# The grouped convolution of a mixer as two plain float32 products side by side, on one Trainium2 core

## What is computed

```python
p = hidden_states @ in_proj_w.T                 # 256 -> 2 x 512
h, gate = (p[..., :I], p[..., I:])
gate = jax.nn.silu(gate)
hc = jnp.transpose(h, (0, 2, 1))
conv = jax.lax.conv_general_dilated(hc, conv_w, window_strides=(1,), padding=[(K - 1, 0)], feature_group_count=G, ...)
h = jnp.transpose(conv + conv_b[None, :, None], (0, 2, 1)) * gate
residual = h
hn = _layernorm(h, ln_g, ln_b)
m = jax.nn.silu(hn @ fc_w.T + fc_b) @ cproj_w.T + cproj_b
return (m + residual) @ out_w.T
```

## Time and profile before

| | |
|---|---|
| runs | 2779.84 us median (2778.41 to 2786.03) |
| the profiled execution's own time | 2780.32 us |
| its span | 2778.2 us |
| mean granted TensorE clock | 0.929 of full speed |
| TensorE busy (matmul) | 2366.8 us, 85% |
| VectorE / ScalarE / GpSimd busy | 1525.3 us (55%) / 1282.9 us (46%) / 518.5 us (19%) |
| mixer stage | from the start to about 764 us |

### The profile page before, as it was taken

The page is one execution under the profiler, slowest core; times in us unless marked ns, Lnnn a source line. Parts: engine busy times, 40 slices in busy tenths (PEclk is TensorE's granted clock), DMA queues, the critical chain, the costliest instruction groups (busy, mean ns, idle before and its releaser), DMA issues. The chain is left out here.

```text
span 2778.2 us, 45597 instructions
## 1 busy us (share of the span) xinstructions
PE 2366.8 (85%) x15266; PEld 1791.3 (64%) x15266; DVE 1525.3 (55%) x3440; ACT 1282.9 (46%) x2197; POOL 518.5 (19%) x429
## 2 busy tenths in 40 slices
PE   7999999999869999647888888888888877159997
PEld 6777777777658888525555555555555557149996
DVE  4544444444345454355666666666666646766664
ACT  2444444444445554624555555555555545024442
POOL 0111111111111111510110000100011013026663
PEclk8999999999989999768999999999999988569998
DMA  3200000000010000122333223223232207435542
GB/s 112 88 0 0 0 0 0 0 0 0 0 31 0 0 0 0 38 69 68 73 75 80 73 74 79 74 70 80 69 77 71 70 24 263 118 111 127 126 89 34
DMA packets 121392, 157.18 MB, mean 57 GB/s; under 512 B 24800, under 2 KB 102000, under 8 KB 121200
## 3 DMA queue, kind: packets, MB, share of 16 engines
q1 hardware_dynamic: 106992, 130.90, 17.2%
q0 software_dynamic: 14336, 25.44, 4.7%
HBM read 96.78 MB, written 58.98 MB: 56 GB/s over the span
## 5 line engine op out<-in xcount | busy, mean ns | idle before, releaser
L1461 DVE TENSOR_REDUCE at_top<-psum 128x1 f32<-128x512 f32 (+3 forms) x1024 | 447.2, 485 | 300.3 <-PE psum L1237 299.7
L1588 ACT ACTIVATE at_probs<-psum 128x512 f32<-128x512 f32 (+1 forms) x768 | 365.8, 530 | 346.5 <-PE psum L1255 344.5
L1235 PE MATMUL psum<-at_k_stack,at_q_stack 96*128 96x512 bf16 (+3 forms) x1024 | 295.4, 315 | 128.0 <-DMA at_k_stack<-qk_parts 72.5
L1253 PE MATMUL psum<-at_q_stack,at_k_stack 98*128 98x512 bf16 (+3 forms) x1024 | 288.9, 309 | 23.1 <-ACT at_probs L1588 16.8
L1235 PEld LDWEIGHTS psum<-at_k_stack,at_q_stack 96*128 96x128 bf16 x1024 | 103.1, 101 | 229.2 <-DVE at_top L1461 102.3
L1237 PE MATMUL psum<-at_mask_q,at_ident_b 128*128 128x128 bf16 x1024 | 206.3, 227 | 0.0
L1255 PE MATMUL psum<-at_mask_k,at_ident_b 128*128 128x128 bf16 x1024 | 202.4, 224 | 0.0
L1253 PEld LDWEIGHTS psum<-at_q_stack,at_k_stack 98*128 98x128 bf16 x1024 | 102.5, 100 | 115.1 <-issue 44.2
L1271 PE MATMUL psum<-at_probs,at_values 128*32 128x512 f32 (+3 forms) x2048 | 151.1, 436 | 0.9 <-ACT at_probs L1588 0.9
L570 POOL TENSOR_TENSOR y<-y,mean 128x512 f32<-128x512 f32 x64 | 83.2, 1333 | 364.8 <-ACT mean L623 364.8
L2312 POOL DMA_INDIRECT out<-ex_result,slot_tokens x64 | 119.6, 1869 | 102.8 <-DVE ex_result L2444 88.2
(11 more groups left out here) (404 smaller groups left out, 6142.1 us busy)
## 6 DMA issues: line engine op xcount, KB each, us to landing
qk_parts<-at_q_parts SPq DMA_DIRECT2D x96, 128.0 KB
qk_parts<-at_k_parts SPq DMA_DIRECT2D x96, 128.0 KB
at_q_stack<-qk_parts SPq DMA_DIRECT2D x64, 192.0 KB
at_k_stack<-qk_parts SPq DMA_DIRECT2D x64, 192.0 KB
x_residual<-in_x SPq DMA_DIRECT2D x16, 512.0 KB, 8.4
at_q_stack<-qk_parts SPq DMA_DIRECT2D x64, 128.0 KB
at_k_stack<-qk_parts SPq DMA_DIRECT2D x64, 128.0 KB
token_rows<-ro_h_tok SPq DMA_DIRECT2D x16, 512.0 KB, 3.0
```

The source lines that it names most:

```text
L1235: pe.matmul(out, q_stack[0:STACK, h, qt * P:(qt + 1) * P], k_stack[0:STACK, h, 0:w], start=True, stop=True)
L1253: pe.matmul(bank(bk)[:, col:col + w], k_stack[0:STACK + N_SHIFT, h, kt * P:(kt + 1) * P], q_stack[0:STACK + N_SHIFT, h, kt * P:T], start=T ...
L1461: dve.tensor_reduce(top[:, h, qt:qt + 1], bank(MAX0 + n % 2)[:, col:col + w], AX.X, ALU.max).then_inc(mxr.sem, 1)
L1588: act.activation(probs[:, slot(h), 512 * f:512 * f + w], bank(f)[:, 0:w], ACT.Exp).then_inc(ex.sem, 1)
```

## The change

The convolution is laid out anew. A new tile `h_taps` holds h in plain float32 twice per block: in copy g the 64 partitions of group g hold h itself, and the other 64 partitions hold the same group's h shifted by one token. One contraction over 128 partitions then covers two taps of one group of 64 channels, and the four taps take two such products per group. The two groups of a block write the two halves of a PSUM bank through two column tiles of TensorE (`tile_position=(0, 64 g)`). ScalarE copies the lower 64 partitions of the product h, once in place and once across to the upper partitions; VectorE does the mirror image. No high and low parts are made for the convolution. Beside this:

- the convolution's weights go by four DMAs straight to their place; their staging area, the two splits and the semaphores of these are gone;
- VectorE computes two of the four pieces of `dev`, GpSimd the other two;
- the narrow matmuls for the squares stand ahead of the first `out` matmul (before: after six), and the `quads` matmul after nine `out` matmuls (before: after twelve);
- VectorE splits `fc` before it copies h, not after;
- batches 4 to 15 of x are loaded one after the other, each when the one before has arrived.

```diff
-        w_conv = pair("w_conv", [P, IK * TAPS, P])
+        w_conv = sb("w_conv", [P, 2 * IK * 2, HALF])
-        h_s = pair("h", [P, IK, TAPS - 1 + T])
+        h_st = sb("h_taps", [P, IK, 2, TAPS - 1 + T])
...
-            sp.dma_start(f_conv, t["conv_blocks"].rearrange("n p m -> p n m")).then_inc(conv_in, 16)
+            for g, side in enumerate(SIDES):
+                for rows, tap in ((SIDES[g], 1), (SIDES[1 - g], 0)):
+                    sp.dma_start(w_conv[rows, 2 * IK * g:2 * IK * (g + 1), :],
+                                 t["conv_blocks"][tap::2, side, side].rearrange("n p m -> p n m")).then_inc(small, 16)
...
-            for b in range(EARLY, NB):
-                load_x(b, x_rest.sem)
+            for i in range(NB):
+                b = i - 1 + EARLY
+                if EARLY <= b < NB:
+                    if b == EARLY:
+                        sp.wait_ge(folded, 1)
+                        sp.wait_ge(mod_done, 2)
+                        sp.wait_ge(lo, len(PIECES))
+                    else:
+                        sp.wait_ge(*x_rest(b - 1 - EARLY, 16))
+                    load_x(b, x_rest.sem)
...
                 if m == 3:
-                    pe.wait_ge(*hl(i, 1))
+                    pe.wait_ge(*ha(i, 2))
+                    pe.wait_ge(*hd(i, 2))
...
             if not first:
-                pe.wait_ge(*hl(i, 3))
+                pe.wait_ge(*ha(i, 6))
+                pe.wait_ge(*hd(i, 6))
                 pe_turn_out(pe, i - 1)
-            pe.wait_ge(*hl(i, 4))
+            pe.wait_ge(*ha(i, 8))
+            pe.wait_ge(*hd(i, 8))
             if first:
-                pe.wait_ge(lo, CONV_W + 1)
+                pe.wait_ge(small, 13 * 16)
...
-                for k in range(TAPS):
-                    last = product3(pe, bank(CONV + m), [w[:, m * TAPS + k, :] for w in w_conv],
-                                    [h[:, m, k:k + T] for h in h_s], k == 0, k == TAPS - 1)
+                for k in range(2):
+                    for g, side in enumerate(SIDES):
+                        last = pe.matmul(bank(CONV + m)[side, :], w_conv[:, 2 * IK * g + 2 * m + k, :],
+                                         h_st[:, m, g, 1 + 2 * k:1 + 2 * k + T], start=(k == 0), stop=(k == 1),
+                                         tile_position=(0, HALF * g), skip_group_check=True)
...
-                    if m == 0 and k == 2:
+                    if m == 0 and k == 0:
                         pe.wait_ge(*sq(i, 4))
...
-                    if m == 1 and k == 0:
+                    if m == 0 and k == 3:
                         pe.wait_ge(*vqs(i, 1))
...
-        def dve_h_lo(dve, i, first):
+        def dve_keep_h(dve, i, first):
             for m in range(IK):
-                dve.wait_ge(*hh(i, m + 1))
-                dve.tensor_tensor(h_s[1][:, m, TAPS - 1:], bank(H0 + m), h_s[0][:, m, TAPS - 1:].bitcast(F32),
-                                  ALU.subtract).then_inc(hl.sem, 1)
+                dve.wait_ge(*hp(i, m + 1))
+                dve.tensor_copy(h_st[SIDES[1], m, 1, TAPS - 1:], bank(H0 + m)[SIDES[1], :]).then_inc(hd.sem, 1)
+                dve.tensor_copy(h_st[SIDES[0], m, 1, TAPS:], bank(H0 + m)[SIDES[1], 0:T - 1]).then_inc(hd.sem, 1)
...
             if not last_batch:
                 dve_hT_lo(dve, i + 1, False)
+            dve.wait_ge(*ms(i, 1))
+            for m in range(2, IK):
+                dve.tensor_tensor(dev[:, m, :], y[:, m, :], mean[:, :], ALU.subtract).then_inc(fc0.sem, 1)
...
-            if not last_batch:
-                dve_h_lo(dve, i + 1, False)
             for m in range(DK):
                 dve.wait_ge(*fh(i, m + 1))
                 dve.tensor_tensor(fc_s[1][:, m, :], fc[:, m, :], fc_s[0][:, m, :].bitcast(F32),
                                   ALU.subtract).then_inc(fl.sem, 1)
+            if not last_batch:
+                dve_keep_h(dve, i + 1, False)
...
-            for m in range(IK):
+            for m in range(2):
                 if m == 0:
                     pool.wait_ge(*ms(i, 1))
                 pool.tensor_tensor(dev[:, m, :], y[:, m, :], mean[:, :], ALU.subtract).then_inc(dv.sem, 1)
...
-                act.activation(h_s[0][:, m, TAPS - 1:], bank(H0 + m), ACT.Copy).then_inc(hh.sem, 1)
+                act.activation(h_st[SIDES[0], m, 0, TAPS - 1:], bank(H0 + m)[SIDES[0], :], ACT.Copy).then_inc(ha.sem, 1)
+                act.activation(h_st[SIDES[1], m, 0, TAPS:], bank(H0 + m)[SIDES[0], 0:T - 1], ACT.Copy).then_inc(ha.sem, 1)
...
-            for m in range(IK):
-                act.wait_ge(*dv(i, m + 1))
+            for m, ready, n in ((2, fc0, 1), (0, dv, 1), (3, fc0, 2), (1, dv, 2)):
+                act.wait_ge(*ready(i, n))
                 act.activation(dev[:, m, :], dev[:, m, :], ACT.Square).then_inc(sq.sem, 1)
```

More of the change, by code:

```diff
@@ L167, in mixer_stage @@
         lnt, hTf, hTh, hTl = signal("ln_turned"), signal("hT_full", DK), signal("hT_hi", DK), signal("hT_lo", DK)
-        hp, hh, hl = signal("h_product", IK), signal("h_hi", IK), signal("h_lo", IK)
+        hp, ha, hd = signal("h_product", IK), signal("h_kept_low", 2 * IK), signal("h_kept_high", 2 * IK)
         gp, gs = signal("gate_product", IK), signal("gate_silu", IK)
         cp, ys, yh, yl = signal("conv_product", IK), signal("y", IK), signal("y_hi", IK), signal("y_lo", IK)
-        mp, ms, dv, sq = signal("mean_product"), signal("mean"), signal("dev", IK), signal("square", IK)
+        mp, ms, sq = signal("mean_product"), signal("mean"), signal("square", IK)
+        dv = signal("dev_pool", 2)
         vqp, vqs, vbp, sd, iv = signal("quad_product"), signal("quad"), signal("var"), signal("std"), signal("inv")
-        fp, fc0, fc1 = signal("fc_product", DK), signal("fc_centred", DK), signal("fc_scaled", DK)
+        fp, fc0, fc1 = signal("fc_product", DK), signal("centred", 2 + DK), signal("fc_scaled", DK)
         fa, fh, fl = signal("fc_silu", DK), signal("fc_hi", DK), signal("fc_lo", DK)
@@ L355, in body @@
                         last.then_inc(vqp.sem, 1)
-                    if m == 1 and k == 0:
+                    if m == 0 and k == 3:
                         pe.wait_ge(*vqs(i, 1))
                         pe.matmul(bank(VB), quads[:, :], quad_sum[:, :], start=True, stop=True).then_inc(vbp.sem, 1)
-                        if not last_batch:
-                            pe.wait_ge(*hTf(i + 1, 1))
+                    if m == 1 and k == 0 and not last_batch:
+                        pe.wait_ge(*hTf(i + 1, 1))
                     product3(pe, bank(OUT + m), [w[:, k, m * P:(m + 1) * P] for w in w_out],
@@ L476, in dve_body @@
                     dve.wait_ge(x_in, 16 * (EARLY - 1))
+                if not isinstance(i, int):
+                    dve.wait_ge(*x_rest(i + 1 - EARLY, 16))
+                    dve.nop(nofuse=True)
                 dve_stats(dve, i + 1)
@@ L515, in dve_body @@
                 dve.wait_ge(*iv(i, 1))
-                dve.wait_ge(*fc0(i, m + 1))
+                dve.wait_ge(*fc0(i, 2 + m + 1))
                 dve.tensor_tensor(fc[:, m, :], fc[:, m, :], inv[:, :], ALU.mult).then_inc(fc1.sem, 1)
-            if not last_batch:
-                dve_h_lo(dve, i + 1, False)
             for m in range(DK):
@@ L523, in dve_body @@
                                   ALU.subtract).then_inc(fl.sem, 1)
+            if not last_batch:
+                dve_keep_h(dve, i + 1, False)
         @block.vector
         def _(dve):
-            for part in h_s:
-                dve.memset(part[:, :, 0:TAPS - 1].bitcast(U32), 0).then_inc(pads.sem, 1)
+            for g in range(2):
+                dve.memset(h_st[SIDES[g], :, g, 0:TAPS - 1], 0.0)
+                dve.memset(h_st[SIDES[1 - g], :, g, 0:TAPS], 0.0)
             dve.memset(mem["neg_half"][:, :], -0.5).then_inc(consts, 1)
@@ L592, in act_hT, with act_keep_h @@
                 act.activation(hT_s[0][:, f, :], hT[:, f, :], ACT.Copy).then_inc(hTh.sem, 1)
-        def act_h_hi(act, i, first):
+        def act_keep_h(act, i, first):
             for m in range(IK):
@@ L658, in _ @@
             act_hi(act, GATE_W)
-            act.wait_ge(conv_in, 16)
-            act_hi(act, CONV_W)
-            act_h_hi(act, 0, True)
+            act_keep_h(act, 0, True)
             act.wait_ge(consts, 5)
-            act.wait_ge(small, 9 * 16)
+            act.wait_ge(small, 13 * 16)
             act_body(act, 0, True, False)
```

40 lines of the change are left out of this document (18 added, 22 removed).

## The result

| | before | after |
|---|---|---|
| median | 2781.24 us (2778.41 to 2786.03, 4 runs) | 2687.21 us (2684.3 to 2689.7, 4 runs) |
| the profiled execution's own time, and its span | 2780.32, 2778.2 us | 2689.7, 2687.9 us |
| mean granted TensorE clock | 0.929 | 0.927 |

The ratio is 0.9659, with a 95% interval of 0.9643 to 0.9675: 3.4% faster. (The 2779.84 us of the table before was the median of the first three runs; with the fourth it is 2781.24.) Predicted were 2687 us with a range of 2675 to 2706.

What follows compares the result with a forecast made beforehand. TensorE was taken to bound the mixer. Fourteen turns at 6.0 us less (38.6 against 44.60) make 84, plus 4.9 in batch 0 and 4.8 in the last: 93.7 off 2780.3, so 2687 us, range 2675 to 2706.

Steps and rivals of the forecast that it cites:

- The convolution: TensorE's convolution in each turn: two column tiles overlapping fully, 7.2 us instead of 11.25, gain 4.05 us in all 16.
- The wait for `fc_lo`: TensorE's wait before `w_comb`: goes once VectorE splits `fc` first, 1.97 us a turn, with 2.4 us to spare.
- The narrow matmuls: TensorE's matmuls for the squares, moved earlier: wait 0.37 us against 0.45 before, counted as nothing; bounds +0.45 and -1.5.
- E: End of the convolution, the zero point from which the prediction counts times in its walk through a new turn.
- Moving half of `dev` to VectorE: Mixer subtractions shared by GpSimd and VectorE: disturbed, two pairs of 1.82 us, last square at E + 8.95; undisturbed E + 8.1.
- The copies: Eight 64-partition copies of h per engine: 0.51 us each on ScalarE, 0.62 or 0.68 on VectorE; neither late.
- the 1 us that I gave `delta`: ScalarE's slack in a turn: it may be 1 us later before TensorE's gate product waits for `delta`.
- Rival 1: A helper becomes late (GpSimd with VectorE, or ScalarE's copies): 15 turns lose 15 to 22 us, 2702 to 2709; chance 0.15.
- The ends: Batches outside the fourteen full turns: batch 0 gains 4.9 us, the last batch 4.8, the prologue nothing.
- The sum: Whole kernel: 84 + 4.9 + 4.8 = 93.7 us less than 2780.3, giving 2686.6.
- Rival 2: Convolution's 64-column tiles do not run together: 14.1 us each, 2797 us in all, slower; chance 0.05.
- Rival 3: No loss for the tiling mode and no GpSimd-VectorE disturbance: 11 us more gain, 2676; chance 0.12.

## Why the prediction was right

Each step against what was measured:

- **The convolution: 7.2 taken, 7.02 measured.** Two tiles of 64 columns overlap fully: 8 x 0.86 = 6.88, and 0.14 is left for the mode where I had 0.34 from the narrow matmuls. The order one group after the other (12.23 us) shows that it is the overlap, and so do the weight loads, two a step against one. Gain 4.23 instead of 4.05.
- **The wait for `fc_lo`: 1.97 taken, 1.96 measured** when it was changed alone. The 2.4 us that it should have to spare are 2.3.
- **The narrow matmuls: a wait of 0.37 taken, 0.89 measured. This step was mis-sized:** I counted nothing for it, and it costs 0.44 a turn, inside its bounds. Price and length of the disturbance were near: VectorE's pieces took 3.48 / 2 = 1.74 us where I took 1.82, GpSimd's 1.55. What was wrong is the order behind it. I set one square behind the last piece; but in the order 2, 0, 3, 1 the piece that comes last is VectorE's second (303.04), and piece 1, done by GpSimd at 302.49, waits behind it. Changing two entries of that table gave the half microsecond. There is also a slip in my sum: its own terms, 4.56 + 3.64 + 0.65, give E + 8.85 and not 8.95, a wait of 0.27; and TensorE came at E + 8.47, 0.11 before my 8.58.
- **Moving half of `dev` to VectorE: priced right, but its alternatives never were.** All on VectorE is 0.8 us a turn better. Against all on GpSimd with the narrow matmuls in their old places the half gained 0.22 us a turn as the kernel stands (38.86 against 39.08), and with the copies in two passes it lost 0.43 (38.85 against 38.42). GPSIMD Engine Reference in the Trainium skill, section Specifications, says that GpSimd shares its SBUF interfaces with VectorE when a VectorE instruction has two SBUF inputs; the trace agrees, with 1.74 us beside GpSimd against 2.49 / 4 = 0.62 alone. I had weighed it only as a price; it was a reason to leave GpSimd out.
- **The copies: 0.51 on ScalarE and 0.62 to 0.68 on VectorE taken, 0.615 and 0.725 measured.** I took the time to go by the 512 columns alone. VectorE: DVE Perf Modes in the Trainium skill, section "Two Vector instructions with no wait between them", states that a Vector instruction whose output starts in another quadrant of 32 partitions than the last output does not start before the earlier ones have finished. The trace agrees: 0.725 when the output goes to and fro, 0.63 in two passes. ScalarE does the same by its rows (0.615 and 0.51). Of the 1 us that I gave `delta`, 0.2 was left. Rival 1 was as near as that: one step on ScalarE.
- **The ends: 9.7 us taken, 9.9 measured, in part by luck.** In batch 0 the narrow matmuls start at 71.11; my walk has 75.4 - 4.05 = 71.35. Two of its steps were off and cancelled. VectorE came to its pieces at 68.16 and not at 73.4 - 4.05 = 69.35, since GpSimd's two pieces were already made and `hT_lo` took 1.28 us and not 2.38; the two subtractions took 1.28 as taken. But the squares begin with VectorE's first piece, so that all four stand behind it, where I had one behind its second:

```profile
68.87 2.19 ACT L650 ACTIVATE y<-y 128x512 f32<-128x512 f32 x4 [4.48 <-DVE y L527]
```

  TensorE waits there 71.11 - 69.67 = 1.44 us, where I had 1.1. The prologue, taken as nothing, gave 0.55: the first convolution starts at 33.13 and not at 33.68. In the last batch `w_comb` waits 4.63 instead of 5.30, as walked through.
- **The sum.** Turns of 38.86 instead of 38.6 make 3.6 us less gain, and the profiled execution is 3.1 above its forecast of 2686.6. That the median of four runs lies on 2687 is partly luck: the profiled execution is the slowest of the four.

Rival 2 (no overlap, slower) is refuted by the timeline; how it would look is the experiment with one group after the other, where the convolution was 12.2 us and the kernel kept hardly any of its gain. Rival 3 was half there: little loss for the mode, but the full disturbance.

The parts don't add up: the order of `fc_lo` alone gives 1.96 us a turn and the convolution alone 3.2 at best (44.60 - 41.4, in turns without the clock), 5.2 together, but the whole change gives 5.74. The copies of the new convolution make VectorE later, so without the new order they lengthen the wait that they stand ahead of.

## What to carry to other kernels

Products that use half of the array's columns halve their time only if the two tiles' matmuls stand one beside the other in the stream, accumulation step by accumulation step. When a bound engine gets shorter, look at the order of the helper's work before its amount: a piece that others wait for goes first, a piece that comes last is used last, and half-partition copies go side by side instead of to and fro. Don't split two-input subtractions between GpSimd and VectorE to save time, where VectorE can make them all in less.

## What the runs showed of the hardware

- Two subtractions of 128 x 512 float32 on VectorE took 3.48 us while GpSimd made two of its own, which took 3.09. Four on VectorE alone took 2.49; four on GpSimd alone 5.16. The pair of engines took 3.6 us for four, a microsecond more than VectorE alone and nearly what the pieces would take one after the other, 2 x 0.62 + 2 x 1.29 = 3.8: side by side the two engines hardly overlap in this work.
- In batch 0 of the changed kernel VectorE's two small operations on 16 elements a partition took as long as GpSimd's two subtractions of 512 that ran beside them, 1.28 us each, where VectorE's other small operations just before took some 0.2. With no subtraction on GpSimd (all four on VectorE) the same two took 0.37 us together. The timeline of VectorE and of GpSimd:

```profile
64.18 0.19 DVE L110 SCALAR_TENSOR_TENSOR mod<-mod,sign 128x32 f32<-128x32 f32 x1
64.48 2.56 DVE L487 TENSOR_SCALAR gate_bias<-mod,out_b 128x16 f32<-128x16 f32 x2
...
68.16 1.28 DVE L527 TENSOR_TENSOR y<-y,mean 128x512 f32<-128x512 f32 x2
```
```profile
64.47 2.54 POOL L593 TENSOR_TENSOR y<-y,mean 128x512 f32<-128x512 f32 x2 [32.41 <-ACT mean L647]
```

- After TensorE had stood for 2.7 us its clock was granted at half for 3 us in six turns of fifteen, and in the others not; after 2.0 us in two of fifteen, after 1.7 us in none. A wait can therefore cost more than its own length.
- ScalarE, too, takes 0.1 us more a copy when its output goes to and fro between the halves of the partitions.
- Eight matmuls of 64 columns on one tile, then eight on the other, took 1.5 us less than sixteen times one: by the weight loads, two matmuls of the second tile had started before the first tile's last ones were through. Alone on its tile such a matmul costs the same 0.86 us as one of 128 columns.
